# Tile-wise differences, a folded own level, and node values made on another engine, in a two-layer model kernel

## The reference, cut to what matters

```python
dt = softplus(x @ Wdt.T + dt_bias);  cg = cumsum(-exp(A_log) * dt, axis=1)
Lam = softplus(Lp * (x @ Wdl.T))                       # per token, head, level
decay = exp(where(t >= s, cg[t] - cg[s], -1e30))
level(t, s) = 0 if s == t else floor(log2(s xor t)) + 1
Wmat = scores * decay * Lam[t, h, level(t, s)]
Y = Wmat @ V;   o = Y @ Wout.T + x;   result = norm(o) * ln_g + ln_b
```

## Time and profile before

| | us |
|---|---|
| median of three runs | 1217.08 |
| lowest, highest | 1216.16, 1217.61 |
| the profiled execution's own time | 1215.93 |
| its span, first to last instruction | 1213.8 |
| PE busy | 1091.7 |
| DVE busy | 1004.4 |
| ACT busy | 691.8 |
| POOL busy | 310.4 |

### The profile page before, as it was taken

How to read it: one execution, slowest core, us unless ns; L and a number is a source line. 1 busy time by engine, 2 the same in 40 slices (tenths; PEclk the granted TensorE clock), 3 DMA queues, 4 the chain that set the end, 5 groups by cost and what they waited for, 6 DMA issues and landing times.

```text
span 1213.8 us, 18006 instructions
## 1 busy us (share of the span) xinstructions
PE 1091.7 (90%) x5756; PEld 665.3 (55%) x5756; DVE 1004.4 (83%) x2141; ACT 691.8 (57%) x1366; POOL 310.4 (26%) x197
## 2 busy tenths in 40 slices
PE   5799989998998989899998989989898998989872
PEld 3455646555564655556465555646555564655641
DVE  4688897979979797997979799797979979797677
ACT  4483845738375573837557283755728375572761
POOL 0050320504114050411405041140504114050273
PEclk9899989899999999999899999999999999999885
DMA  3000000000000000000000000000000000001136
GB/s 133 9 9 10 1 18 9 17 9 0 17 9 17 9 17 9 0 17 9 17 9 17 9 0 17 9 17 9 17 9 0 17 9 17 9 17 54 67 101 203
DMA packets 32562, 28.64 MB, mean 24 GB/s; under 512 B 1568, under 2 KB 26144, under 8 KB 32288
## 3 DMA queue, kind: packets, MB, share of 16 engines
q1 hardware_dynamic: 32544, 28.42, 7.2%
HBM read 16.09 MB, written 12.32 MB: 23 GB/s over the span
## 4 chain that ended last, share of the span: by engine, by line
PE 45%; DVE 37%; issue 11%; ACT 5%; DMA 1%; DVEq 0%; ACTq 0%; SPq 0%; POOLq 0%; POOL 0%
DVE ms L1256 6%; PE p L581 4%; PE p L619 3%; DVE skip L1088 3%; PE p L544 3%; PE p L556 2%; PE p L570 2%; DVE pair L1329 2%; DVE nodesT L1265 2%; PE p L433 2%; PE p L394 2%; ACT vdw L849 2%; PE p L424 2%; DVE pair L1323 2%; DVE y L1168 2%
## 5 line engine op out<-in xcount | busy, mean ns | idle before, releaser
L1516 POOL TENSOR_TENSOR pair<-pair,cgt 128x2048 f32<-128x2048 f32 x16 | 58.4, 3647 | 772.5 <-DVE pair L1316 772.5
L858 ACT ACTIVATE gx<-p 128x512 f32<-128x512 f32 x256 | 143.4, 591 | 13.9 <-PE p L479 8.2
L477 PE MATMUL p<-x1Th,Gl 128*128 128x512 f32 x256 | 120.1, 469 | 4.0 <-ACT gx L858 4.0
L813 ACT ACTIVATE gelu<-p,bias_u 128x512 f32<-128x512 f32 x32 | 22.0, 687 | 151.3 <-PE p L424 151.3
L479 PE MATMUL p<-x1Th,Gh 128*128 128x512 f32 x256 | 102.1, 399 | 0.0
L478 PE MATMUL p<-x1Tl,Gh 128*128 128x512 f32 x256 | 101.8, 398 | 0.0
L1529 POOL TENSOR_TENSOR vp<-vdw,beta 128x384 f32<-128x384 f32 (+3 forms) x80 | 80.9, 1042 | 56.0 <-DVE beta L1308 56.0
L544 PE MATMUL p<-gx,x1T 128*32 128x512 f32 x512 | 77.2, 679 | 12.8 <-DVE pair L1333 12.0
L581 PEld LDWEIGHTS p<-vbd,pair 128*128 128x128 f32 x512 | 62.0, 191 | 42.9 <-issue 31.0
L1256 DVE TENSOR_TENSOR ms<-lam,K 128x64 f32<-128x64 f32 (+4 forms) x80 | 84.5, 1132 | 0.0
L394 PE MATMUL p<-xnT,MC 128*128 128x512 f32 x64 | 42.6, 756 | 46.4 <-DVE y L1161 46.4
(11 more groups left out here) (239 smaller groups left out, 2705.3 us busy)
## 6 DMA issues: line engine op xcount, KB each, us to landing
xin<-in_x SPq DMA_DIRECT2D x16, 256.0 KB, 2.8
hx_scratch<-vdw SPq DMA_DIRECT2D x16, 256.0 KB, 2.5
res_scratch<-res SPq DMA_DIRECT2D x15, 256.0 KB, 2.0
W<-in_weights SPq DMA_DIRECT2D x1, 1477.5 KB, 9.3
gx<-hx_scratch SPq DMA_DIRECT2D x5, 256.0 KB, 4.5
out<-gx SPq DMA_DIRECT2D x5, 256.0 KB, 2.7
gx<-in_weights SPq DMA_DIRECT2D x1, 1216.0 KB, 11.7
GT<-hx_scratch SPq DMA_DIRECT2D x4, 256.0 KB, 4.1
```

What stands on the lines that cost most here:

```text
L477: pe.matmul(head_bank(h)[:, :], tile(Gl, h), x1Th[:, :], start=True, stop=False)
L858: act.activation(tile(gx, h, T), head_bank(h)[:, :], ACT.Copy).then_inc(R["gx_copied"], 1)
```

## The change

Five edits. The pair differences are made tile by tile (four instructions of 512 columns for one of 2048), and ScalarE's Abs and Exp as well. The own level is no longer an array of its own: `fold_own`, three new VectorE instructions on lam (384, 320 and 320 columns), puts level 0 into the level values of the nodes, with coefficients that `node_vectors` makes once in the prologue (17 small steps), so that the matrix product of `pair_levels` yields level 0 on the diagonal too; line 1329's add and `own_level` go. The node values move from VectorE to GpSimd, ahead of `level_values` (five products and a copy). TensorE does the first `pair_levels` ahead of `left_halves`. `norm2` moves behind the second tile's `pair_weights`, and writes over `skip`, where the attention's output now is.

```diff
@@ buffers
-        self_lam = sb("self_lam", TILES * 512)
+        lam_own = sb("lam_own", 64 * 6)
+        member = sb("member", NODES)
+        left_t = sb("left_t", 128)
+        rbit = sb("rbit", 5)
+        ones_to = sb("ones_to", 6)
+        own_coef = sb("own_coef", 6)
-        yt, ytT, ob = rs[:, 0:T], rs[:, T:2 * T], rs[:, 2 * T:3 * T]
+        yt, ytT, ob = rs[:, 0:T], rs[:, T:2 * T], skip
@@ TensorE, stages()
                     pair_scores(i, 0)
+                    pair_levels(i, 0)
                     left_halves(i)
-                    pair_levels(i, 0)
                     node_matrices(i)
@@ ScalarE
             def pair_decay(i):
-                act.wait_ge(R["diff_ready"], i + 1)
-                act.activation(pair[:, :], pair[:, :], ACT.Abs).then_inc(R["diff_abs"], 1)
-                act.wait_ge(R["diff_abs"], i + 1)
-                act.activation(pair[:, :], pair[:, :], ACT.Exp, scale=-1.0).then_inc(R["decay_ready"], 1)
+                for n in range(TILES):
+                    act.wait_ge(R["diff_ready"], 4 * i + n + 1)
+                    act.activation(tile(pair, n, 512), tile(pair, n, 512), ACT.Abs).then_inc(R["diff_abs"], 1)
+                for n in range(TILES):
+                    act.wait_ge(R["diff_abs"], 4 * i + n + 1)
+                    act.activation(tile(pair, n, 512), tile(pair, n, 512), ACT.Exp, scale=-1.0).then_inc(R["decay_ready"], 1)
             def left_halves(i):
                 if later(i):
-                    act.wait_ge(R["n_ready"], i)
+                    act.wait_ge(R["ob_ready"], i)
+                    act.wait_ge(R["c_ready"], B if isinstance(i, int) else i)
@@ VectorE
+            def node_vectors():
+                step(dve.transpose(left_t[:, :], k("left")))
+                step(dve.tensor_reduce(member[:, :], view(left_t[:, :], "p (c n) -> p n c", c=4), AX.X, ALU.add))
+                step(dve.tensor_tensor(member[:, :], member[:, :], k("right"), ALU.add))
...
+                step(dve.scalar_tensor_tensor(own_coef[:, 0:5], ones_to[:, 1:6], -2.0, ones_to[:, 0:5], ALU.mult, ALU.add))
+                step(dve.tensor_copy(own_coef[:, 5:6], ones_to[:, 5:6]))
+                step(dve.scalar_tensor_tensor(left, spread(k("own_chunk").unsqueeze(2), [128, 4, CHUNK]), k("diag", 31, 32),
+                                              left, ALU.mult, ALU.add))
-            def node_lams(i):
-                for level in range(5, 0, -1):
-                    count = (CHUNK >> level) + (level == 1)
-                    last = dve.tensor_tensor(nd[:, :, at:at + count], spread(l[:, :, level:level + 1], [128, 64, count]),
-                                             spread(k("right", at, at + count).unsqueeze(1), [128, 64, count]), ALU.mult)
+            def fold_own(i):
+                dve.wait_ge(R["lam_ready"], i + 1)
+                if later(i):
+                    dve.wait_ge(R["nodes_ready"], i)
+                dve.tensor_tensor(own, spread(l[:, :, 0:1], [128, 64, 6]),
+                                  spread(own_coef[:, :].unsqueeze(1), [128, 64, 6]), ALU.mult).then_inc(R["own_steps"], 1)
+                dve.tensor_tensor(l[:, :, 1:6], l[:, :, 1:6],
+                                  spread(rbit[:, :].unsqueeze(1), [128, 64, 5]), ALU.mult).then_inc(R["own_steps"], 1)
+                dve.wait_ge(R["own_steps"], 2 * i + 2)
+                dve.tensor_tensor(l[:, :, 1:6], l[:, :, 1:6], own[:, :, 0:5], ALU.add).then_inc(R["lamx_ready"], 1)
             def pair_weights(i, n):
-                if n == 0:
-                    dve.wait_ge(R["decay_ready"], i + 1)
+                dve.wait_ge(R["decay_ready"], 4 * i + n + 1)
                 dve.wait_ge(R["lam_ps"], 4 * i + n + 1)
                 dve.tensor_tensor(tile(pair, n, 512), tile(pair, n, 512), P1[2][:, :], ALU.mult)\
                     .then_inc(R["dlam_ready"], 1)
-                dve.tensor_tensor(tile(pair, n, 512), tile(pair, n, 512), tile(self_lam, n, 512), ALU.add)\
-                    .then_inc(R["lams_ready"], 1)
                 dve.wait_ge(R["s_ps"], 4 * i + n + 1)
@@ VectorE, stages()
                     level_factors(i)
                     lam_sum(i)
+                    fold_own(i)
...
                     level_weights(i)
                     if later(i):
                         stats2(i - 1)
-                    node_lams(i)
...
-                    if later(i):
-                        norm2(i - 1)
                     node_rows(i)
...
                     own_heads(i, 0)
                     pair_weights(i, 1)
+                    if later(i):
+                        norm2(i - 1)
                     level_sum(i, 0)
@@ VectorE, prologue
                     heads_low_part()
+                    node_vectors()
@@ GpSimd
-            def own_level(i):
-                pool.tensor_tensor(view(self_lam[:, :], "p (m t) -> p m t", t=CHUNK),
-                                   spread(view(lam[:, :], "p (m l) -> p m l", l=LEVELS)[:, :, 0:1], [128, 64, CHUNK]),
-                                   spread(k("diag").unsqueeze(1), [128, 64, CHUNK]), ALU.mult).then_inc(R["self_ready"], 1)
+            def node_lams(i):
+                pool.wait_ge(R["lamx_ready"], i + 1)
+                for level in range(5, 0, -1):
+                    count = CHUNK >> level
+                    pool.tensor_tensor(nd[:, :, at:at + count], spread(l[:, :, level:level + 1], [128, 64, count]),
+                                       spread(member[:, at:at + count].unsqueeze(1), [128, 64, count]), ALU.mult)
+                pool.tensor_copy(nd[:, :, at:at + 1], own[:, :, 5:6]).then_inc(R["nodes_ready"], 1)
             def pair_differences(i):
-                pw = view(pair[:, :], "p (m t) -> p m t", t=CHUNK)
-                pool.tensor_tensor(pw, pw, spread(cgt[:, :].unsqueeze(2), [128, 64, CHUNK]), ALU.subtract)\
-                    .then_inc(R["diff_ready"], 1)
+                for n in range(TILES):
+                    pw = view(tile(pair, n, 512), "p (m t) -> p m t", t=CHUNK)
+                    pool.tensor_tensor(pw, pw, spread(cgt[:, H * n:H * n + H].unsqueeze(2), [128, H, CHUNK]), ALU.subtract)\
+                        .then_inc(R["diff_ready"], 1)
                 pair_differences(i)
+                node_lams(i)
                 level_values(i)
-                own_level(i)
                 if later(i):
                     finish(i - 1)
```

More of the change, by code:

```diff
@@ L1067, in before, with step @@
                 dve.wait_ge(R["setup_done"], 3)
+            def node_vectors():
+                steps = [0]
+                def step(ins):
+                    steps[0] += 1
+                    ins.then_inc(R["basis"], 1)
+                    dve.wait_ge(R["basis"], steps[0])
+                step(dve.transpose(left_t[:, :], k("left")))
+                step(dve.tensor_reduce(member[:, :], view(left_t[:, :], "p (c n) -> p n c", c=4), AX.X, ALU.add))
+                step(dve.tensor_tensor(member[:, :], member[:, :], k("right"), ALU.add))
+                at = 0
+                for level in range(5, 0, -1):
+                    count = CHUNK >> level
+                    step(dve.tensor_reduce(rbit[:, level - 1:level], k("right", at, at + count), AX.X, ALU.add))
+                    at += count
+                step(dve.memset(ones_to[:, 0:1], 1.0))
+                for level in range(1, 6):
+                    step(dve.tensor_tensor(ones_to[:, level:level + 1], ones_to[:, level - 1:level],
+                                           rbit[:, level - 1:level], ALU.mult))
+                step(dve.scalar_tensor_tensor(own_coef[:, 0:5], ones_to[:, 1:6], -2.0, ones_to[:, 0:5], ALU.mult, ALU.add))
+                step(dve.tensor_copy(own_coef[:, 5:6], ones_to[:, 5:6]))
+                left = view(k("left"), "p (c s) -> p c s", c=4)
+                step(dve.scalar_tensor_tensor(left, spread(k("own_chunk").unsqueeze(2), [128, 4, CHUNK]), k("diag", 31, 32),
+                                              left, ALU.mult, ALU.add))
             def heads_low_part():
@@ L1500, in residual @@
                                    spread(w("lnbias").unsqueeze(1), [128, TILES, D]), ALU.add).then_inc(R["res_init"], 1)
-            def own_level(i):
-                pool.wait_ge(R["lam_ready"], i + 1)
+            def node_lams(i):
+                pool.wait_ge(R["lamx_ready"], i + 1)
                 if later(i):
-                    pool.wait_ge(R["lams_ready"], 4 * i)
-                pool.tensor_tensor(view(self_lam[:, :], "p (m t) -> p m t", t=CHUNK),
-                                   spread(view(lam[:, :], "p (m l) -> p m l", l=LEVELS)[:, :, 0:1], [128, 64, CHUNK]),
-                                   spread(k("diag").unsqueeze(1), [128, 64, CHUNK]), ALU.mult).then_inc(R["self_ready"], 1)
+                    pool.wait_ge(R["c_ready"], B if isinstance(i, int) else i)
+                if later(i):
+                    pool.wait_ge(R["lev_ps"], 4 * i)
+                l = view(lam[:, :], "p (m l) -> p m l", l=LEVELS)
```

(9 more changed lines are left out.)

23 lines of the change are left out of this document (7 added, 16 removed).

## The result

The changed kernel took 1250.54 us (median of 4 runs, 1247.85 to 1253.24), the kernel before 1217.34 in the same series (4 runs, 1216.16 to 1219.0). The ratio is 1.026, with a 95% interval of 1.023 to 1.028: slower by 33 us, where the forecast was 46. The profiled execution took 1253.24 us with a span of 1251.4 (before: 1215.93 and 1213.8).

The account below looks back on a forecast made before the run. TensorE from line 581 on was taken as the bound, with ScalarE's order a hidden second. 14 x (1.7 + 1.7) = 47.6, +1.3 prologue, -2 first, -1 last round: +46 on 1217, 1263 us; range 1200 to 1288.

Parts of the forecast that it names:

- Steps 1 to 3: VectorE and GpSimd, start of round: tile-wise differences, fold and GpSimd nodes alternate on the shared port; second-norm statistics 4.8 us late.
- Step 4: VectorE's scan inputs start at 510.6 against 510.80, so TensorE's scan wait of 2.96 us stays (2.8).
- Step 5: ScalarE: rstd2 waits for the late statistics, Abs and Exp take 4.4 us, line 918's copies start 4.6 us late.
- Step 6: TensorE: node_matrices waits for ScalarE's copies, chunk_values starts at 526.5 against 524.65; +1.7 us per round.
- 73 to 75 us given as a sign: The length of a loop round expected in the changed trace if the forecast holds.
- Step 7: TensorE's clock: a second idle stretch brings a stretch at clock 0.50; bounds nothing to 3.4 us, taken 1.7 per round.
- Step 8: Line 1329's add gone and norm2 moved: off the path in the loop, -2 us first round, -1 last round.
- Step 9: Prologue: node_vectors' 17 dependent steps ahead of line 1192, which idled 2.60 us; +0.8 to +2.5, taken 1.3 us.
- small stall: Rival: steps 1 to 6 hold but no clock loss, +22 us, 1239; chance 0.14.
- "faster" rival: Rival: no alternation on the port, statistics end before 507, line 581 starts near 523.5; 1199 us, chance 0.14.

Follow-up runs that it names:

- experiment 2: Changed kernel with the node products (five and a copy) back on VectorE, behind the second norm's statistics: 1249.68 us, ratio 1.025.
- experiment 5: Changed kernel with GpSimd's level values ahead of its node products and TensorE's left_halves ahead of the first pair_levels: 1216.48 us, ratio 0.999.
- experiment 1: Changed kernel with ScalarE's second-norm reciprocal deviation (rstd2) moved behind the copies of node_matrices: 1216.17 us, ratio 0.998.
- experiment 10: Kernel before the change with one edit, the second norm's statistics ahead of level_factors on VectorE: 1206.68 us, ratio 0.990.
- experiment 6: Changed kernel with fold_own behind level_weights instead of ahead of the delta sum: 1263.74 us, ratio 1.037.
- experiment 8: Changed kernel with nodes on VectorE behind the scan inputs, second norm's statistics ahead of level_factors, left_halves ahead of the first pair_levels: 1174.87 us, ratio 0.965.
- experiment 3: Changed kernel with differences, Abs and Exp of the pair array as one instruction each again: 1233.54 us, ratio 1.011.
- experiment 4: Changed kernel with the second norm's statistics ahead of level_factors on VectorE instead of behind level_weights: 1213.47 us, ratio 0.995.
- experiment 7: Changed kernel, nodes still on GpSimd, with statistics and level values first, fold_own behind scan inputs, Abs and Exp whole, own_values earlier, TensorE reordered: 1223.1 us, ratio 1.004.
- experiment 9: As experiment 8, with fold_own behind the scan inputs, Abs and Exp whole, own_values ahead of ScalarE's last head copies: 1164.01 us, ratio 0.956.

## Why the prediction was right, step by step

Forecast +46, measured +33; the sign, the mechanism and the range held. The nearness of the sum is in part luck. In the two profiled executions the 14 rounds of the loop became 26.7 us longer (47.6 said), the prologue 5.7 (1.3 said), the first round 1.4 (2 less said), and the stretch from the last round's start to the end 3.8 (1 less said): the loop falls 20.9 us short of its term, and the three others together are 12.6 above theirs.

- Steps 1 to 3 (alternation, late statistics). Statistics 5.1 us later in the round (4.8 said); nodes and alpha products share their stretch, and experiments 2 and 5 show the alpha products back at 0.78 us without the nodes beside them. Held and shown.
- Step 4 (TensorE's scan wait stays, 2.8): 2.84 us. Held.
- Step 5 (ScalarE). `rstd2` is at 13.32 us of the round instead of 8.25, +5.1; Abs and Exp take 4.26 us (4.4 said); the copies of line 924 are 4.2 us late (4.6 said). Held; experiment 1 shows that the order behind this wait makes the loss.
- Step 6 (+1.7 us a round). `chunk_values` at 28.85 us (28.86 said), the quicker round 72.46 us against 70.91: +1.55. Held, though these rounds lie below the 73 to 75 us given as a sign. Some rounds of before were longer than 70.91 already (the second by 3.7 us, three by 0.4 to 0.5), which the sum left out: 5 us.
- Step 7 (clock, +1.7 a round). This is the term that was mis-sized. A second stretch at clock 0.50 exists and costs 1.61 us where it falls (the difference between the two rounds), but it falls in six of the 14 rounds only: 9.7 us in all where the sum has 23.8, so 14 us too many. The bounds, nothing and 3.4 a round, held it; my 1.7 took its own size for its mean. What it was reasoned from was off too: not some 4 us of idle time ahead of `node_matrices`, but 0.62 and 0.58 in the quicker round and 0.99 and 0.58 in the longer one. The earlier low stretch fell on the work ahead of it, which so ended at 607.8, 22.0 us into the round, and not at 19.7.
- Step 8 (-2 in the first round, -1 in the last). Wrong in both: the first round is 1.4 us longer, and the stretch from the last round's start to the end 3.8 us. The second round is 2.1 us shorter, but for another reason: the 8.54 us of node products beside `own_level`, shown in experiment 10. What the late ScalarE and the add of line 1329 each did in the first and the last round I did not separate; that stays open.
- Step 9 (`node_vectors`, +1.3). In this execution it is hidden: VectorE still waits 2.62 us behind it.

```profile
51.92 0.35 DVE L1099 SCALAR_TENSOR_TENSOR K<-K 128x128 f32<-128x128 f32 x1
54.89 0.69 DVE L1225 TENSOR_TENSOR x<-p,xin 128x512 f32<-128x512 f32 x1 [2.62 <-PE p L442]
...
41.80:52.00 10.20, 9.28 (x23) 4.86 (x23) 9.41 (x25) 2.66 (x3) 0.00 (x0) 0.50 0.00 0
```

The third row shows what hides it: TensorE ran 10.2 us of the prologue at clock 0.50. In the profiles of experiments 1, 2, 6 and 8, whose prologues have the same code and run this part at full clock, VectorE doesn't wait behind it. Experiment 6:

```profile
50.80 0.35 DVE L1099 SCALAR_TENSOR_TENSOR K<-K 128x128 f32<-128x128 f32 x1
51.18 0.69 DVE L1225 TENSOR_TENSOR x<-p,xin 128x512 f32<-128x512 f32 x1
```

From the start of VectorE's last instruction ahead of `node_vectors` (45.15) to line 1225 these are 6.03 us, against 4.88 before (44.60 to 49.48): +1.1, so the term held where it can be seen. The first difference comes at 72.70 and 71.81 in experiments 1 and 6, and at 76.37 in the profile of the changed kernel. Over the ten profiles with this prologue it lies between 71.8 and 76.4; what decides on it stays open. So some 4 us of the profiled 37.6 belong to this execution and not to the change; the medians differ by 33.

Of the rivals, "small stall" (1239) was the nearest to what most rounds show, and experiment 3 gave it almost in full (1233.5). The "faster" rival's condition, statistics done early, was met in experiment 4; experiment 1 reaches the same for ScalarE with the statistics late. Its price was wrong. It gave 1199, they 1213 and 1216, since the nodes (0.79 us in both) and the level values (0.87 us in experiment 4) hold TensorE next. My own expectations for experiments 4 to 7 made the same mistake four times: each followed one wait to its end and took the next one in another engine's queue for absent. Only with the nodes out of GpSimd's queue and the other late inputs moved ahead (experiments 8 and 9), with no TensorE wait above 1.4 us left in the round, did the time drop clearly.

## What to carry to other kernels

Work that leaves one engine may bring nothing if both engines go on taking turns at the same moment; look at what the freed engine runs in that stretch, and at who stands behind its next result. An engine busy 56% of the time can be a bound by its order alone: moving one late-fed entry of ScalarE's queue behind work that was ready gave 34 us. And after removing a wait, price the next late input on every engine before believing the gain.

## What the chip showed unexpectedly

- The low clock depends on small differences: with 5.7 us of ScalarE's wait in both, the tile-wise kernel has a second stretch at clock 0.50 in six of 14 rounds (74.07 us instead of 72.46), the whole-tile kernel (rounds of 71.97 us) in none. What sets the alternation stays open. In the kernels of experiments 8 and 9, with no TensorE wait above 1.4 us in the rounds shown, the clock is 1.00 throughout them. In experiment 4, whose longest is 1.59 us, it is so in all rounds of the loop but one; behind the scan wait of 2.8 to 3.0 us a low stretch comes in most rounds.
- GpSimd's time for the same five node instructions (1984 columns) is 4.64 us with VectorE idle, 4.67 beside VectorE's four short alpha products, and 6.47 beside its later, longer work (experiment 7); VectorE does them in 3.04 us when mostly undisturbed and in 5.05 to 5.14 beside GpSimd's level values. The four alpha products take 0.78 us undisturbed and 4.39 beside the nodes. So in these stretches the engine with the short instructions loses most by the turns.
